# Residual blocks of the experts' norm brought into the PSUM banks by the transposing form of the matmul

## What is computed

```python
cms_out = gelu(attn_out @ cW1 + cb1) @ cW2 + cb2 + target_embed
concat = concatenate([attn_out, cms_out], axis=-1)
modifier = gelu(concat @ mW1 + mb1) @ mW2 + mb2
hidden_states = clip(x + cms_out + modifier, 0.0, 1.0)
...
residual = hidden_states                       # (8, 256, 512)
h = einsum('bsh,bhk->bsk', hidden_states, Wd) + bd[:, None, :]
h = gelu(h)
h = einsum('bsk,bkh->bsh', h, Wu) + bu[:, None, :]
h = residual + h
mean = mean(h, axis=-1, keepdims=True)
var = mean(square(h - mean), axis=-1, keepdims=True)
h = (h - mean) * rsqrt(var + LN_EPS)
return h * g[:, None, :] + b[:, None, :]
```

## Time and profile before

| | |
|---|---|
| median of 3 runs | 1086.0 us (1083.89 to 1086.42) |
| the profiled execution | 1083.45 us |
| its span, first to last instruction | 1081.7 us |
| around the span | 1.75 us |
| PE busy | 1050.0 us (97%) |
| DVE busy | 801.1 us (74%) |
| ACT busy | 511.4 us (47%) |
| TensorE clock granted, mean | 0.998 |

### The profile page before, as it was taken

One profiled execution on the slowest core, in us unless ns is written; L12 is line 12 of the kernel. 1 busy time (PEld: TensorE's weight loads), 2 busy tenths in 40 slices (PEclk: granted clock), 3 DMA queues, 4 the chain that ended last, 5 costly groups with the idle time before them and its releaser, 6 DMA issues. The chain is left out here.

```text
span 1081.7 us, 13978 instructions
## 1 busy us (share of the span) xinstructions
PE 1050.0 (97%) x4986; PEld 873.9 (81%) x4986; DVE 801.1 (74%) x1402; ACT 511.4 (47%) x913; POOL 6.4 (1%) x15
## 2 busy tenths in 40 slices
PE   8999999999999999999999999999999999999996
PEld 7889778888877788888789877888887778888885
DVE  4435986776588887877675698677658888877787
ACT  4425855444265444333565385454425554343462
POOL 0000000000000000000000000000000000000001
PEclk9999999999999999999999999999999999999999
DMA  5600221210142232303653122312013323332042
GB/s 202 228 1 12 68 77 40 78 40 20 59 175 98 92 143 78 136 20 109 242 170 101 43 78 79 117 40 78 20 58 124 130 98 121 113 137 79 29 146 78
DMA packets 54718, 101.61 MB, mean 94 GB/s; under 512 B 3102, under 2 KB 31866, under 8 KB 50810
## 3 DMA queue, kind: packets, MB, share of 16 engines
q1 hardware_dynamic: 54560, 100.70, 26.7%
q10 hardware_dynamic: 90, 0.02, 0.0%
HBM read 79.74 MB, written 20.97 MB: 93 GB/s over the span
## 5 line engine op out<-in xcount | busy, mean ns | idle before, releaser
L1045 DVE TENSOR_TENSOR acc<-bank,acc 128x512 f32<-128x512 f32 x224 | 154.1, 688 | 85.1 <-PE bank L218 85.0
L216 PE MATMUL bank<-hid_hi,w_lo 128*128 128x512 f32 x512 | 200.5, 392 | 6.7 <-DVE hid_lo L934 3.7
L633 ACT ACTIVATE sbc<-sbc,bias 128x512 f32<-128x512 f32 x112 | 80.8, 724 | 254.7 <-DVE sbc L1015 193.2
L217 PE MATMUL bank<-hid_hi,w_hi 128*128 128x512 f32 x512 | 199.3, 389 | 0.0
L218 PE MATMUL bank<-hid_lo,w_hi 128*128 128x512 f32 x512 | 199.2, 389 | 0.0
L216 PE MATMUL bank<-ta_hi,w_lo 128*128 128x512 f32 x448 | 175.8, 392 | 5.1 <-DVE ta_lo L934 2.0
L218 PE MATMUL bank<-ta_lo,w_hi 128*128 128x512 f32 x448 | 174.4, 389 | 0.0
L217 PE MATMUL bank<-ta_hi,w_hi 128*128 128x512 f32 x448 | 174.4, 389 | 0.0
L1015 DVE TENSOR_TENSOR sbc<-bank,sbc 128x512 f32<-128x512 f32 x144 | 98.1, 686 | 41.5 <-PE bank L218 41.4
L216 PEld LDWEIGHTS bank<-hid_hi,w_lo 128*128 128x128 f32 x512 | 96.1, 188 | 31.4 <-DVE w_lo L934 3.6
L218 PEld LDWEIGHTS bank<-hid_lo,w_hi 128*128 128x128 f32 x512 | 96.1, 188 | 20.0
(11 more groups left out here) (215 smaller groups left out, 1552.0 us busy)
## 6 DMA issues: line engine op xcount, KB each, us to landing
w_raw<-in_L_cond_mW SPq DMA_DIRECT2D x48, 512.0 KB, 3.4
w_raw<-in_L_cond_cW SPq DMA_DIRECT2D x32, 512.0 KB, 4.4
pre_d<-sbc SPq DMA_DIRECT2D x10, 1024.0 KB, 3.9
sbc<-pre_d SPq DMA_DIRECT2D x10, 1024.0 KB, 7.3
x_raw<-in_x SPq DMA_DIRECT2D x4, 1024.0 KB, 6.3
e_raw<-in_L_cond_W_down SPq DMA_DIRECT2D x8, 512.0 KB, 5.4
e_raw<-in_L_cond_W_up SPq DMA_DIRECT2D x8, 512.0 KB, 4.5
out<-acc SPq DMA_DIRECT2D x16, 256.0 KB, 2.1
```

Of the source, the lines that this page charges most:

```text
L216: nc.tensor.matmul(dst, w_l, a_h, start=start, stop=False, **kw)
L217: nc.tensor.matmul(dst, w_h, a_h, start=False, stop=False, **kw)
L633: nc.scalar.activation(dst, dst, ACT.Gelu, **kw).then_inc(g_done[key], 1)
L1045: nc.vector.tensor_tensor(dst, bank[:, :], dst, ALU.add).then_inc(evac, 1)
```

## The change

The matmul at L440 gets `is_transpose=True`. Operands, banks, order, waits and signals stay; the instructions of all engines stand in the same order in both programs.

```diff
@@ -439,7 +439,7 @@
                 for k in range(KT):
                     nc.tensor.matmul(ps[b0 + t][:, k * P:(k + 1) * P],
                                      acc[:, k, pp * TB + t * P:pp * TB + (t + 1) * P], ident[:, :],
-                                     start=k == 0, stop=True, skip_group_check=True)
+                                     is_transpose=True, start=k == 0, stop=True, skip_group_check=True)
             pe.wait_ge(h3_l, 2 * n + 2)
```

## The result

The changed kernel takes 1081.67 us (median of 6 runs, 1080.18 to 1081.94) against 1086.11 us for the kernel before (6 runs, 1083.79 to 1086.42). The ratio is 0.9965, with a 95% interval from 0.9955 to 0.9975: 3.8 us faster, between 2.7 and 4.9. Forecast were 1082.3 us and 3.66 us.

A forecast was written before the change was run, and what follows sets the result against it. PE was taken as the bound around the two middle pe_up calls. Two savings of 1.83 us there and zero at the end made 3.66 us, so 1086.0 - 3.66 = 1082.3 us, range 1079.5 to 1084.7 us.

The forecast's parts named there:

- The price of a call: At L440, 16 blocks of one pe_up call take 1.66 us instead of 3.49, saving 1.83 us of PE.
- The lower bound of the gain: The prologue's run of 16 transposing blocks took 3.44 us; at that price nothing is saved.
- The middle calls: Calls 0 and 1 of pe_up: both savings of 1.83 us count fully, 3.66 us on the path.
- the 4.57 us of slack: From ACT's first exponential ending at 572.05 to pair 2's values on PE at 576.62, set against 1.83 us.
- Rival 1: A fixed date in batch 1's attention absorbs one middle saving; 1.83 us stay, 1084.2 us; chance 0.10.
- The end: Calls 2 and 3 of pe_up: DVE's norms have dates from ACT and DVE itself, so the gain is zero.
- the cover is thin the other way: At the last two calls, a block run more than some 0.4 us longer would be paid at the end.
- The sum: 3.66 us off the profiled execution, giving 1079.8 us, and off the median, giving 1082.3 us, a gain of 0.34%.
- Rival 2: All four pe_up calls count, 7.3 us saved, 1078.7 us; chance 0.04.
- rival 3: Nothing changes at L440: still two passes, or the spacing of the prologue's run; 1086.0 us; chance 0.05.
- Rivals 4 and 5: Slower: in the middle calls the clock falls (1097 us, chance 0.04), or blocks are spaced by duration (1087.8 us, chance 0.03).

The follow-up runs named there:

- the run of 80: Changed kernel with the 16 transposing blocks of each middle call done five times: 1095.59 us against 1080.09 us for the changed kernel on the same chip.
- second profile of the changed kernel: Another profiled execution of the same changed kernel, without the clock fall at 526 us; span 1077.8 us, 3.9 us under that of the kernel before.
- the doubled plain blocks: Kernel before with the plain blocks of pairs 2 and 3, at the end, each done a second time: 1092.49 us, ratio 1.0062.
- the two runs that split the calls: Kernel before with the flag in the two middle calls alone, 1080.26 us, ratio 0.9955; and in the two end calls alone, 1085.16 us, ratio 0.9998.

## Why the prediction was right

**The price of a call** was taken from L354, 1.66 us against 3.49 us. Measured were 1.66 and 1.67 us. The count of records, two passes for a plain block and one for a transposing one, was the sound part of the argument; the durations of 275 and 273 ns would have shown no difference at all. The lower bound of the gain, the prologue's 3.44 us, fits the lower level of the clock: 215 ns a block, twice the distance of a run at L354. The clock column prints 1.00 there all the same (the kernel before, columns as in the earlier trace rows), so the distance between starts has to confirm the column, as it does at L354 and in the run of 80:

```profile
4.00:6.00 2.00, 2.00 (x12) 2.00 (x10) 0.00 (x0) 0.00 (x0) 0.00 (x0) 1.00 1.05 358
```

**The middle calls** were said to be fully on the path, with the norm of pair 1 at 594.9 us. In the second profile of the changed kernel (PE at the values of pair 2, then DVE):

```profile
574.79 0.40 PE L216 MATMUL bank<-aw_hi,x_lo 128*128 128x512 f32 x1
...
594.88 0.70 DVE L1157 BATCH_NORM_STATS2 stat<-bank 128x6 f32<-128x512 f32 x1 [0.78 <-PE bank L218]
596.15 0.70 DVE L1157 BATCH_NORM_STATS2 stat<-bank 128x6 f32<-128x512 f32 x1 [0.57 <-PE bank L218]
```

The first call's saving came out of the 4.57 us of slack, as the step said: the values start 1.83 us earlier than in the earlier trace rows, and DVE, which starts the norm of pair 0 at 562.22 us in both profiles, did not hold PE up. At the norm of pair 1, where DVE had waited 2.60 us in the earlier trace rows, 0.78 are left: the second call's 1.83 us came out of this wait, and the first call's had moved DVE's own work ahead of it, as the step said. Rival 1 would have shown a wait of zero. In the same profile PE is still busy throughout, 75.30 us of the window from 553 to 628.3 us, and its waits up to 630 us are the old one alone (the window row, then the row of waits):

```profile
553.00:628.30 75.30, 75.30 (x471) 67.82 (x469) 54.31 (x115) 42.18 (x82) 2.78 (x4) 1.00 0.34 101
```

```profile
PE bank L216 <- DVE ta_lo L934: 1.0, 1, 1.0
```

**The end** was put at zero gain, and the run with the flag there alone gave 0.9998. The remark that the cover is thin the other way was tested too; the estimate drawn from it, 6.5 us for the doubled plain blocks, lies inside what was measured, and the trace has 6.2.

**The sum**, 3.66 us, lies inside the interval of each comparison of the full change. The median came out 0.6 us under the forecast of 1082.3. The medians of the full change moved by 4.4 and 4.9 us, which is more than the calls can give: the kernel before spreads over 4 us on one chip, and a median takes in how many of its runs lost time at 526 us and in the prologue. That the forecast of the median came so near is in part luck. What the prediction missed is these two places. I had put the 2.55 us between the profiled execution and the median down as given, and had read a profile without the fall as if it stood for all runs. I had also taken 3.3 us for the least gain that can be told from no change; the interval came out 1.1 us to either side of 3.8.

**The rivals.** Rival 2 fell with the two runs that split the calls, rival 3 with the record count. Rival 1 fell with the flag in the middle alone and with the wait of 0.78 us. Rivals 4 and 5 fell twice, in the changed kernel and in the run with 80 blocks in a row. The Trainium skill's sentences behind these two ("TensorE: Matmul & The Clock Gate", Part 4: PE-mode transpose) do not price this change. The page's 275 ns, given for bf16, agrees with the recorded duration of one fp32 block, 272 ns here, but blocks start 104 to 108 ns apart. The page also says that full clock doesn't engage for transposes; 8.65 us of them behind dense matmuls did not let it fall here, the clock stayed at 1.00. By the spacing of the blocks the clock also rose while PE ran nothing else. In the prologue PE runs nothing but transposing blocks before its first 512-column matmul, and they change from 215 ns apart to 104 ns apart on the way. In the profile with plain matmuls at L354, whose prologue is that of the kernel before, PE reads:

```profile
7.90 3.39 PE L228 MATMUL bank<-ident,wk_raw 128*128 128x128 f32 x16
11.13 1.91 PE L228 MATMUL bank<-ident,wv_raw 128*128 128x128 f32 x16
12.79 0.48 PE L216 MATMUL bank<-wt_hi,wt_lo 128*128 128x512 f32 x1
```

The last 16 blocks take 12.79 - 11.13 = 1.66 us, the time of a run at full clock.

## What to carry to other kernels

A plain fp32 matmul with the identity is two passes on TensorE where the transposing form is one; count the records of the group and compare the distance between starts, since the durations hide it. Before booking a saving on the busiest engine, ask at each place who takes its result and what that engine waits for just before: here half of the saved TensorE time lay where the norm's engine had its dates from elsewhere. And look for gaps of TensorE ahead of dense work when the runs of one kernel spread: a few throw-away matmuls in such a gap went with steadier times here.

## What the runs showed of the hardware

- fp32r matmuls that add to a bank just filled by transposing blocks keep the pace that they had behind the plain ones: the first of them is recorded with 0.47 to 0.48 us in both forms.
- TensorE's clock fell to 0.50 after an idle time of 2.19 us in five of eight profiles and not in the others: it cost about 1.6 us in the first profile of the changed kernel, and the profile shown before has the same idle time and no fall. I had looked for such a fall only at the transposes.
- At the end of the kernel before the clock column falls too, to 0.50 once PE has finished (from 1077 us on), and this costs nothing, as no matmul is left. The mean clock of an execution is therefore no sign of a loss by itself: it is 0.998 in the profile before and 0.996 in the second one of the changed kernel, and neither has the fall at 526 us.
- In the prologue fp32 transposing blocks start 215 ns apart at first and 104 ns apart from about 11 us on in the profile with plain matmuls at L354, with nothing but such blocks on PE until then. The clock column prints 1.00 in the prologue of the kernel before too, also where its blocks start 215 ns apart.
